# Gate and up projections copied out of PSUM by ACT and multiplied by GpSimd, in place of DVE, in a fused attention and SwiGLU kernel

## The chip, the cores and the metric

One core of one Trainium2 chip. The time is that of the whole kernel on the device, in microseconds (us); lower is better. The engines are TensorE (PE in the profile; its weight loads are PEld), DVE (VectorE), ACT (ScalarE), POOL (GpSimd) and SP (SyncE, which here issues DMAs).

## The reference, cut to what matters

The input is 4 batches of 1024 tokens with 128 channels. A layer norm without weights is shared by an attention branch and a feed-forward branch, and both are added to the input.

```python
xn = (x - mean) / sqrt(var + 1e-5)
# attention: 16 heads of 8 channels, 4 key/value heads, rope, softmax over all 1024 keys
q, k, v = xn @ Wq.T + bq, xn @ Wk.T + bk, xn @ Wv.T + bv
q, k = rope(q), rope(k)
context = softmax(q @ k.T / sqrt(8)) @ v
attention = context @ Wo.T + bo
# feed-forward: weights are integers times 1/127, 384 hidden channels
gate, up = xn @ wg.T, xn @ wu.T
ffn = (silu(gate) * up) @ wd.T
out = x + attention + ffn
```

The kernel forms silu by a tanh: silu(gate) = 0.5 * gate * (1 + tanh(gate / 2)).

## The kernel before

**Groups.** The attention is cut into 16 groups (NG): one batch and one key/value head each, with its 4 query heads. Each group has two passes over the scores. The first finds the maximum of each row: 64 units (AU), each a TensorE matmul of 128 queries by 512 keys into a PSUM bank (`max_unit`, L796) and a DVE reduce out of that bank (`reduce_max`, L640). The second computes the scores transposed, with the negative maxima as extra rows of the matmul (`scores`, L813), takes the exponential on ACT (`exps`, L487) and multiplies by v on TensorE (`weigh`, L882: eight records of a step, called a value batch below).

**Steps.** A group has 16 steps. In a step TensorE issues four max units, which run ahead of their use by 48 units (LEAD), four score matmuls of the next step and one value batch; ACT takes four exponentials; DVE takes four reduces. All engines follow one order written out by hand (`step_order`, L74, from the table `JOB_AT`, L67), in which further jobs are placed:

```python
JOB_AT = {1: (UP, 0), 3: (UP, 1), 5: (NEG_T, 1), 7: (UP, 2), 8: (CTX, 0), 10: (DOWN, 0), 13: (NEG_T, 0), 16: (CTX, 1)}
```

In a step, TensorE's order is max and score matmuls in turn (three of each), the job, the value batch, then the fourth max unit and the fourth score matmul. ACT's order is three exponentials, its part of the job, the fourth exponential.

**The feed-forward jobs.** Each group also does a sixteenth of the feed-forward branch: 256 tokens (CH) and three chunks of 128 hidden channels (FC). UP (`ffn_gate_up`, L888) puts gate in the first and up in the second half of a PSUM bank; ACT writes tanh(gate / 2) to SBUF (L536); DVE's `hidden` (L677 to L684) then makes two instructions that read the bank: gated = (th + 1) * gate (L680) and hid = 0.5 * gated * up (L683). DOWN (`ffn_down_proj`, L897) multiplies the three chunks of hid by the down weights, and DVE adds the result into `y_all` (`add_ffn`, L690).

**The split of the maximum.** When 32 reduces (half a group, HU) are done, DVE negates the row maxima and splits them into three bf16 parts in five small instructions on 128x16 tiles in SBUF, `split_neg`: L651, L655, L657, L660, L662, one behind each of five reduces. L651 has two SBUF inputs. TensorE transposes the parts (`transpose_neg`, L801, job NEG_T), ACT copies them (L478) and SP stores them into the rows of `qc`. The half that job (NEG_T, 1) needs is complete with the fourth reduce of step 3, the one that (NEG_T, 0) needs with the fourth reduce of step 11 (which belongs to the next group).

**Banks.** Jobs and max units share a ring of four PSUM banks (`bank`, L185). Before TensorE takes a bank, `bank_left` (L926) waits for the last reader of what stood in it four places before: for a max unit that is its reduce, for UP it was the second product, `hid_done` (L931). Score matmuls have three banks of their own.

**POOL.** Besides work ahead of the groups, POOL splits the rotated queries of batches 1, 2 and 3 into three bf16 parts: `split_later` (L383 to L405) has seven instructions on 128x1024 tiles in SBUF (L388, L389, L391, L397, L399, L401, L403), and three DMAs (L427) store them. The batches run one behind the other in the loop of L424, beside group 0 and in front of all of POOL's per-group work. That work is `group` (L432): wait for the group's last value batch, then copy v for the group after next (`copy_v`, L411).

**Loops.** Groups 0 to 13 run in a hardware loop of seven iterations with two groups each (even, then odd), so there are six returns to its start. Groups 14 and 15 are written out. The last group has no max units of a next one and does the output projection of the last batches beside it.

Of the kernel before, what the change touches and what calls it, by code (L numbers as in the profile page):

```python
# [16 lines left out]
HID = 384  # L17
# [92 lines left out]
def attention_swiglu(nc, x, wf, wi, biases, bo, tables, identity, out):  # L110
# [3 lines left out]
    with ExitStack() as ctx:  # L114
# [3 lines left out]
        def sem(name):  # L118
            return ctx.enter_context(nc.semaphore(name))
# [31 lines left out]
        neg_max_T = sb("neg_max_T", [PARTS * G * HT, P], BF16)  # L151
        th = sb("th", [P, FC, CH])
        gated = sb("gated", [P, FC, CH])
        hid = sb("hid", [P, FC, CH])
# [92 lines left out]
        ffn_up = sem("ffn_up")  # L247
        tanh_done = sem("tanh_done")
        gated_done = sem("gated_done")
# [123 lines left out]
        def _(pool):  # L373
# [3 lines left out]
            pool.wait_ge(ones_set, 4)  # L377
            pool.sem_inc(q_stored, 1)
            for b, n in ((1, 2), (2, 3)):
                pool.wait_ge(rstd_done, n)  # L380
                normalise(pool, nc.gpsimd, b, xn_done_pool)
# [41 lines left out]

            for b in range(1, B):  # L424
                split_later(b)
                for n in range(PARTS):
                    pool.dma_start(q_parts[b * KV:(b + 1) * KV, :, n, :, :].rearrange("g j d t -> (g j) d t"),  # L427
                                   part[:, (b + 1) % 2, n, :]).then_inc(q_dma, 16)
                pool.wait_ge(q_dma, 16 * PARTS * b)
                pool.sem_inc(q_stored, 2)  # L430

            def group(g, par):  # L432
                pool.wait_ge(pv_done, STEPS * (g + 1) + SLOTS)
                copy_v(g + 2, par)

            with pool.Fori(0, NG // 2 - 1) as pair:
                group(pair * 2, 0)
                group(pair * 2 + 1, 1)


        @block.scalar
        def _(act):
# [83 lines left out]
            def group(g, left):  # L526
                slot = 0
                for s in range(1, STEPS + (left > 1)):
                    after = (g + (s + 1) // STEPS, (s + 1) % STEPS)
                    more = s + 1 < STEPS or left > 1  # L530
                    if more:
                        exps(*after, range(G - 1))
                    for kind, n in step_order(s, left == 1):
                        if kind == UP:
                            act.wait_ge(ffn_up, FC * g + n + 1)
                            nc.scalar.activation(th[:, n, :], bank(slot)[:, 0:CH], ACT.Tanh,  # L536
                                                 scale=0.5).then_inc(tanh_done, 1)
                        if kind == NEG_T:
                            copy_neg(g + 1 - n, n, bank(slot))
                        slot += 1  # L540
                    if more:
                        exps(*after, [G - 1])
                    if s % NT == NT - 1:
                        act.wait_ge(pv_done, STEPS * g + s + 1 + SLOTS)
                        nc.scalar.activation(acc_sb[:, s // NT, :], acc_ps[:, :], ACT.Copy).then_inc(acc_copied, 1)  # L545
# [11 lines left out]
        def _(dve):  # L557
# [75 lines left out]
            dve.wait_ge(ffn_in, 16)  # L633
            nc.vector.tensor_scalar(w_ffn[:, :], wi_sb[:, :], DEQUANT, None, ALU.mult).then_inc(w_done, 1)

# [40 lines left out]

            def hidden(g, c, ps):  # L677

                dve.wait_ge(tanh_done, FC * g + c + 1)
                nc.vector.scalar_tensor_tensor(gated[:, c, :], th[:, c, :], 1.0, ps[:, 0:CH], ALU.add,  # L680
                                               ALU.mult).then_inc(gated_done, 1)
                dve.wait_ge(gated_done, FC * g + c + 1)
                nc.vector.scalar_tensor_tensor(hid[:, c, :], gated[:, c, :], 0.5, ps[:, CH:2 * CH],  # L683
                                               ALU.mult, ALU.mult).then_inc(hid_done, 1)  # L684

            def add_ffn(g, ps):
                dve.wait_ge(bo_added, B)
                dve.wait_ge(ffn_down, g + 1)
                chunk = y_all[:, bass.ds(g * CT, CT), :]
                nc.vector.tensor_tensor(chunk, chunk, ps[:, 0:CT * D].rearrange("p (t d) -> p t d", t=CT),  # L690
                                        ALU.add).then_inc(y_done, 1)
# [20 lines left out]
            def job(g, slot, kind, n):  # L712
                ps = bank(slot)
                if kind == UP:
                    hidden(g, n, ps)
                elif kind == DOWN:
                    add_ffn(g, ps)
# [24 lines left out]
        def _(pe):  # L742
            pe.sem_inc(pv_done, SLOTS)
            pe.wait_ge(w_in, 32)

# [121 lines left out]
            pe.wait_ge(raw_done, 2 * B)  # L867
            pe.wait_ge(w_done, 1)
            pe.wait_ge(qc_loaded[0], DMAS_C)
# [23 lines left out]
            def ffn_down_proj(g, ps):  # L893
                pe.wait_ge(hid_done, FC * (g + 1))
                for t in range(CT):
# [30 lines left out]
            def bank_left(g, kind, n, back=0):  # L926
# [3 lines left out]
                elif kind == UP:  # L930
                    pe.wait_ge(hid_done, FC * g + n + 1 - FC * back)  # L931
                elif kind == DOWN:
# [139 lines left out]
```

## Time and profile before

| | |
|---|---|
| median of 3 runs | 880.38 us |
| lowest and highest | 879.12, 881.32 us |
| the profiled execution | 878.84 us, with a span of 877.0 us |
| busy share of the span | PE 90%, DVE 86%, ACT 68%, PEld 29%, POOL 10% |
| chain that ended last, by engine | PE 61%, DVE 14%, issue 13%, ACT 9% |
| mean granted TensorE clock | 0.953 of full speed |

Times are microseconds from the start of the span unless marked ns. In the timeline a row is one instruction, or several of one group merged (xcount), with its start and its duration; in square brackets stands how long its engine had been idle before it and which engine's instruction released it, where that is known. Merged rows overlap with what runs between their parts. The matmuls are pipelined, so that the durations of neighbours overlap; the distance of two starts says more than a duration. The line number is that of the kernel, and line numbers below are those of the kernel before.

### The profile page before, as it was taken

To read this page: it belongs to the slowest core of one execution; us is meant where nothing else is said; L and a number is where in the kernel's file an instruction comes from. 1 tells how busy PE (TensorE), PEld (TensorE's weight loads), DVE (VectorE), ACT (ScalarE), POOL (GpSimd) and SP (SyncE) were. 2 spreads that over 40 slices of the span, in tenths; PEclk is the share of its full clock that TensorE was granted. 3 is DMA by queue.
4 is the path that set the end of the run, shared out by engine and by line. 5 is a ranking of instruction groups with operands and counts; after the bars stand their busy time and mean duration, and the time that the engine had idled before them with its cause. 6 is when DMAs were issued, how large, how long until landed. Compare 5 with 4: busy or idle time off the path is not lost.

```text
span 877.0 us, 18027 instructions
## 1 busy us (share of the span) xinstructions
PE 790.0 (90%) x4856; PEld 253.0 (29%) x4856; DVE 752.4 (86%) x1486; ACT 595.1 (68%) x1171; POOL 84.2 (10%) x81
## 2 busy tenths in 40 slices
PE   3697699989999899989999899989999899999996
PEld 2221232323322232323322232323223222323252
DVE  7687989979999699979999799979998899999931
ACT  2433477777777577767777577767777677777764
POOL 4169770000000000000000000000000000000000
PEclk9695899999999899999999899989999999999999
DMA  6302222011010101011010000110010000100021
GB/s 194 90 1 63 65 66 64 29 30 27 9 44 6 28 27 28 28 30 27 18 38 6 25 27 28 28 30 27 19 36 9 26 24 27 28 27 2 2 61 37
DMA packets 29220, 30.35 MB, mean 35 GB/s; under 512 B 6672, under 2 KB 21264, under 8 KB 29008
## 3 DMA queue, kind: packets, MB, share of 16 engines
q1 hardware_dynamic: 27552, 25.05, 10.0%
q0 software_dynamic: 720, 2.36, 1.0%
q10 hardware_dynamic: 864, 2.15, 0.7%
q14 instruction: 72, 0.59, 0.2%
q8 instruction: 12, 0.20, 0.1%
HBM read 23.12 MB, written 6.03 MB: 33 GB/s over the span
## 4 chain that ended last, share of the span: by engine, by line
PE 61%; DVE 14%; issue 13%; ACT 9%; SPq 1%; DVEq 1%; DMA 1%; ACTq 1%
PE acc_ps L882 24%; PE banks L796 13%; PE banks L813 8%; DVE mx L640 8%; ACT probs L487 6%; PE banks L888 5%; PE banks L897 3%; PE banks L905 2%; ACT acc_sb L545 2%; DVE neg_max L662 1%; PE banks L922 1%; DVE rest L657 1%; PE banks L801 1%; DVE neg_max L660 1%; PE banks L772 1%
## 5 line engine op out<-in xcount | busy, mean ns | idle before, releaser
L640 DVE TENSOR_REDUCE mx<-banks 128x1 f32<-128x512 f32 x1024 | 639.4, 682 | 56.1 <-PE banks L796 40.5
L487 ACT ACTIVATE probs<-banks 128x512 f32<-128x512 f32 x1024 | 536.9, 603 | 210.4 <-PE banks L813 193.5
L813 PE MATMUL banks<-qc,kc 51*128 51x512 bf16 x1024 | 324.9, 392 | 18.8 <-ACT probs L487 8.7
L796 PE MATMUL banks<-ka,qa 48*128 48x512 bf16 x1024 | 297.7, 394 | 26.6 <-DVE mx L640 11.3
L882 PE MATMUL acc_ps<-probs,v_grp 128*32 128x512 f32 x2048 | 279.8, 619 | 0.7 <-ACT probs L487 0.7
L796 PEld LDWEIGHTS banks<-ka,qa 48*128 48x128 bf16 x1024 | 77.9, 95 | 337.6 <-DVE mx L640 263.2
L813 PEld LDWEIGHTS banks<-qc,kc 51*128 51x128 bf16 x1024 | 79.1, 94 | 134.6 <-ACT probs L487 129.7
L411 POOL COPY v_grp<-v_all 128x64 f32 (+1 forms) x16 | 3.7, 238 | 636.5 <-PE acc_ps L882 636.5
L888 PE MATMUL banks<-xn_T,w_ffn 128*128 (+1 forms) x192 | 57.8, 426 | 0.0
L882 PEld LDWEIGHTS acc_ps<-probs,v_grp 128*32 128x32 f32 x2048 | 40.7, 109 | 57.9 <-issue 47.0
L680 DVE SCALAR_TENSOR_TENSOR gated<-th,banks 128x256 f32<-128x256 f32 x48 | 20.2, 421 | 23.0 <-ACT th L536 19.5
L888 PEld LDWEIGHTS banks<-xn_T,w_ffn 128*128 128x128 f32 x192 | 34.8, 202 | 15.3 <-issue 11.8
L905 PE MATMUL banks<-ident,acc_sb 128*128 128x128 f32 x128 | 20.1, 280 | 7.5 <-ACT acc_sb L545 7.5
L897 PE MATMUL banks<-w_ffn,hid 128*128 128x128 f32 x192 | 25.7, 284 | 0.0
L897 PEld LDWEIGHTS banks<-w_ffn,hid 128*128 128x128 f32 x192 | 22.6, 191 | 3.8 <-issue 3.8
L536 ACT ACTIVATE th<-banks 128x256 f32<-128x256 f32 x48 | 18.4, 383 | 7.6 <-PE banks L888 5.1
L683 DVE SCALAR_TENSOR_TENSOR hid<-gated,banks 128x256 f32<-128x256 f32 x48 | 20.2, 421 | 1.6
L766 PE MATMUL banks<-xn_T,wf_sb 128*128 128x512 f32 x32 | 20.7, 770 | 0.7 <-ACT xn_T L458 0.7
L545 ACT ACTIVATE acc_sb<-acc_ps 128x512 f32<-128x512 f32 x32 | 18.9, 591 | 1.2 <-PE acc_ps L882 1.2
L801 PE MATMUL banks<-ident,neg_max 128*96 128x128 bf16 x32 | 8.2, 257 | 12.2 <-DVE neg_max L662 12.2
L905 PEld LDWEIGHTS banks<-ident,acc_sb 128*128 128x128 f32 x128 | 13.4, 140 | 16.9 <-issue 16.9
L760 PE MATMUL banks<-ident,xn 128*128 128x128 f32 x16 | 4.4, 433 | 14.3 <-DVE xn L278 10.4
(85 smaller groups left out, 270.7 us busy)
## 6 DMA issues: line engine op xcount, KB each, us to landing
qa<-q_parts SPq DMA_DIRECT2D x32, 96.0 KB
qc<-q_parts SPq DMA_DIRECT2D x64, 48.0 KB
q_parts<-part POOLq DMA_DIRECT2D x9, 256.0 KB, 3.8
y_all<-in_x SPq DMA_DIRECT2D x4, 512.0 KB, 9.3
qa<-q_parts SPq DMA_DIRECT2D x32, 64.0 KB
qc<-q_parts SPq DMA_DIRECT2D x64, 32.0 KB
out<-y_all SPq DMA_DIRECT2D x8, 256.0 KB, 2.3
ka<-k_parts SPq DMA_DIRECT2D x32, 48.0 KB
```

What stands on the lines that cost most here:

```text
L487: nc.scalar.activation(probs[:, s % SLOTS, j, :], banks[:, score_bank(G * s + j), :], ACT.Exp, scale=SCALE).then_inc(exp_done, 1)
L545: nc.scalar.activation(acc_sb[:, s // NT, :], acc_ps[:, :], ACT.Copy).then_inc(acc_copied, 1)
L640: nc.vector.tensor_reduce(out=mx[:, h, col, k:k + 1], in_=ps, op=ALU.max, axis=AX.X).then_inc(max_done, 1)
L680: nc.vector.scalar_tensor_tensor(gated[:, c, :], th[:, c, :], 1.0, ps[:, 0:CH], ALU.add, ALU.mult).then_inc(gated_done, 1)
L683: nc.vector.scalar_tensor_tensor(hid[:, c, :], gated[:, c, :], 0.5, ps[:, CH:2 * CH], ALU.mult, ALU.mult).then_inc(hid_done, 1)
L766: return nc.tensor.matmul(s_ps[:, n, h, :], wf_sb[:, c + n * D:c + (n + 1) * D], xn_T[:, b * T + h * W:b * T + (h + 1) * W], start=True, s ...
L796: nc.tensor.matmul(ps, qa[par][rows, j // 2, t * P:(t + 1) * P], ka[par][rows, k * W:(k + 1) * W], start=True, stop=True).then_inc(a_ready, 1)
L813: nc.tensor.matmul(banks[:, score_bank(u), :], kc[par][rows, kt * P:(kt + 1) * P], qc[par][rows, h, j // 2, :], start=True, stop=True).the ...
L882: last = nc.tensor.matmul(acc_ps[VC * j:VC * (j + 1), :], v_grp[par][:, kt, :], probs[:, s % SLOTS, j, :], start=(kt == 0), stop=(kt == NT ...
L888: last = nc.tensor.matmul(ps[:, n * CH:(n + 1) * CH], w_ffn[:, n * HID + c * P:n * HID + (c + 1) * P], xn_T[:, bass.ds(g * CH, CH)], start ...
L897: last = nc.tensor.matmul(ps[:, t * D:(t + 1) * D], hid[:, c, t * P:(t + 1) * P], w_ffn[:, 2 * HID + c * D:2 * HID + (c + 1) * D], start=( ...
L905: last = nc.tensor.transpose(ps[:, t * P:(t + 1) * P], acc_sb[:, h, t * P:(t + 1) * P], ident[:, :])
```

## The change

ACT waits until the hidden tile of the group before is made, then writes its tanh as before, and behind it copies the whole bank (gate and up, 128x512) to a new SBUF tile `gu`. Both count on one semaphore, `gu_done`, and TensorE may take the bank again when both are done. The products move from DVE to POOL as three instructions on 128x256 tiles, all in SBUF: gated = gate * up, th = th * gated, hid = th + gated. The factor 0.5 moves into the dequantised down weights, which makes two DVE instructions of one there. DVE keeps only the add of the down projection. `th` is now written again by POOL.

On POOL, the per-group function now has the three chunks first, then (in groups 0, 1 and 2) one of the batches 1, 2 and 3, then the wait and the copy of v. The first four groups are written out, ten run in a loop of five iterations, and the last two are written out without the copy. `hid_done` and `ffn_down` start from a first count so that the waits for the group before pass in group 0.

```diff
--- before.py
+++ after.py
@@ -150,6 +150,7 @@
         neg_max = sb("neg_max", [P, 2 * 2, PARTS, PAIRS * HT], BF16)
         neg_max_T = sb("neg_max_T", [PARTS * G * HT, P], BF16)
         th = sb("th", [P, FC, CH])
+        gu = sb("gu", [P, FC, 2 * CH])
         gated = sb("gated", [P, FC, CH])
         hid = sb("hid", [P, FC, CH])
         rec = sb("rec", [P, NH, HT, G])
@@ -245,7 +246,7 @@
         pv_done = sem("pv_done")
         acc_copied = sem("acc_copied")
         ffn_up = sem("ffn_up")
-        tanh_done = sem("tanh_done")
+        gu_done = sem("gu_done")
         gated_done = sem("gated_done")
         hid_done = sem("hid_done")
         ffn_down = sem("ffn_down")
@@ -376,6 +377,7 @@
                     nc.gpsimd.memset(kc[i][e * E_ROWS + 32:(e + 1) * E_ROWS, :], 1.0).then_inc(ones_set, 1)
             pool.wait_ge(ones_set, 4)
             pool.sem_inc(q_stored, 1)
+            pool.sem_inc(hid_done, FC)
             for b, n in ((1, 2), (2, 3)):
                 pool.wait_ge(rstd_done, n)
                 normalise(pool, nc.gpsimd, b, xn_done_pool)
@@ -421,7 +423,7 @@
                                         bo_sb[:, :].unsqueeze(1).to_broadcast([P, NT, D]),
                                         ALU.add).then_inc(bo_added, 1)
 
-            for b in range(1, B):
+            def later(b):
                 split_later(b)
                 for n in range(PARTS):
                     pool.dma_start(q_parts[b * KV:(b + 1) * KV, :, n, :, :].rearrange("g j d t -> (g j) d t"),
@@ -429,13 +431,34 @@
                 pool.wait_ge(q_dma, 16 * PARTS * b)
                 pool.sem_inc(q_stored, 2)
 
-            def group(g, par):
-                pool.wait_ge(pv_done, STEPS * (g + 1) + SLOTS)
-                copy_v(g + 2, par)
-
-            with pool.Fori(0, NG // 2 - 1) as pair:
-                group(pair * 2, 0)
-                group(pair * 2 + 1, 1)
+            def hidden(g, c):
+
+                if c == 0:
+                    pool.wait_ge(ffn_down, g + 1)
+                pool.wait_ge(gu_done, 2 * (FC * g + c + 1))
+                nc.gpsimd.tensor_tensor(gated[:, c, :], gu[:, c, 0:CH], gu[:, c, CH:2 * CH],
+                                        ALU.mult).then_inc(gated_done, 1)
+                pool.wait_ge(gated_done, 2 * (FC * g + c) + 1)
+                nc.gpsimd.tensor_tensor(th[:, c, :], th[:, c, :], gated[:, c, :], ALU.mult).then_inc(gated_done, 1)
+                pool.wait_ge(gated_done, 2 * (FC * g + c) + 2)
+                nc.gpsimd.tensor_tensor(hid[:, c, :], th[:, c, :], gated[:, c, :], ALU.add).then_inc(hid_done, 1)
+
+            def group(g, par, batch=None, more=True):
+                for c in range(FC):
+                    hidden(g, c)
+                if batch is not None:
+                    later(batch)
+                if more:
+                    pool.wait_ge(pv_done, STEPS * (g + 1) + SLOTS)
+                    copy_v(g + 2, par)
+
+            for g in range(KV):
+                group(g, g % 2, batch=g + 1 if g + 1 < B else None)
+            with pool.Fori(0, NG // 2 - 3) as pair:
+                group(pair * 2 + KV, 0)
+                group(pair * 2 + KV + 1, 1)
+            group(NG - 2, 0, more=False)
+            group(NG - 1, 1, more=False)
 
 
         @block.scalar
@@ -532,9 +555,11 @@
                         exps(*after, range(G - 1))
                     for kind, n in step_order(s, left == 1):
                         if kind == UP:
+                            act.wait_ge(hid_done, FC * g + n + 1)
                             act.wait_ge(ffn_up, FC * g + n + 1)
                             nc.scalar.activation(th[:, n, :], bank(slot)[:, 0:CH], ACT.Tanh,
-                                                 scale=0.5).then_inc(tanh_done, 1)
+                                                 scale=0.5).then_inc(gu_done, 1)
+                            nc.scalar.activation(gu[:, n, :], bank(slot), ACT.Copy).then_inc(gu_done, 1)
                         if kind == NEG_T:
                             copy_neg(g + 1 - n, n, bank(slot))
                         slot += 1
@@ -631,7 +656,8 @@
             root(slice(2 * NT, NTT), 2)
             nc.vector.tensor_copy(ident16[:, :], ident[:, :]).then_inc(id_done, 1)
             dve.wait_ge(ffn_in, 16)
-            nc.vector.tensor_scalar(w_ffn[:, :], wi_sb[:, :], DEQUANT, None, ALU.mult).then_inc(w_done, 1)
+            for n, scale in ((slice(0, 2 * HID), DEQUANT), (slice(2 * HID, 3 * HID), 0.5 * DEQUANT)):
+                nc.vector.tensor_scalar(w_ffn[:, n], wi_sb[:, n], scale, None, ALU.mult).then_inc(w_done, 1)
 
             def reduce_max(g, a, ps):
                 dve.wait_ge(a_ready, AU * g + a + 1)
@@ -674,18 +700,9 @@
             for a in range(LEAD):
                 maximum(0, a, first_bank(first_slot(a)))
 
-            def hidden(g, c, ps):
-
-                dve.wait_ge(tanh_done, FC * g + c + 1)
-                nc.vector.scalar_tensor_tensor(gated[:, c, :], th[:, c, :], 1.0, ps[:, 0:CH], ALU.add,
-                                               ALU.mult).then_inc(gated_done, 1)
-                dve.wait_ge(gated_done, FC * g + c + 1)
-                nc.vector.scalar_tensor_tensor(hid[:, c, :], gated[:, c, :], 0.5, ps[:, CH:2 * CH],
-                                               ALU.mult, ALU.mult).then_inc(hid_done, 1)
-
             def add_ffn(g, ps):
                 dve.wait_ge(bo_added, B)
-                dve.wait_ge(ffn_down, g + 1)
+                dve.wait_ge(ffn_down, g + 2)
                 chunk = y_all[:, bass.ds(g * CT, CT), :]
                 nc.vector.tensor_tensor(chunk, chunk, ps[:, 0:CT * D].rearrange("p (t d) -> p t d", t=CT),
                                         ALU.add).then_inc(y_done, 1)
@@ -711,9 +728,7 @@
 
             def job(g, slot, kind, n):
                 ps = bank(slot)
-                if kind == UP:
-                    hidden(g, n, ps)
-                elif kind == DOWN:
+                if kind == DOWN:
                     add_ffn(g, ps)
                 elif kind == CTX:
                     normalise_context(g, n, ps)
@@ -741,6 +756,7 @@
         @block.tensor
         def _(pe):
             pe.sem_inc(pv_done, SLOTS)
+            pe.sem_inc(ffn_down, 1)
             pe.wait_ge(w_in, 32)
 
             def transpose_xn(b, h):
@@ -865,7 +881,7 @@
                     pe.wait_ge(max_done, a - 1)
                     transpose_neg(0, 0, first_bank(NEG_BEHIND + 1))
             pe.wait_ge(raw_done, 2 * B)
-            pe.wait_ge(w_done, 1)
+            pe.wait_ge(w_done, 2)
             pe.wait_ge(qc_loaded[0], DMAS_C)
             for j in range(G):
                 scores(0, 0, 0, j)
@@ -891,7 +907,7 @@
                 last.then_inc(ffn_up, 1)
 
             def ffn_down_proj(g, ps):
-                pe.wait_ge(hid_done, FC * (g + 1))
+                pe.wait_ge(hid_done, FC * (g + 2))
                 for t in range(CT):
                     for c in range(FC):
                         last = nc.tensor.matmul(ps[:, t * D:(t + 1) * D], hid[:, c, t * P:(t + 1) * P],
@@ -928,7 +944,7 @@
                 if kind == MAX:
                     pe.wait_ge(max_done, AU * g + n + 1 - AU * back)
                 elif kind == UP:
-                    pe.wait_ge(hid_done, FC * g + n + 1 - FC * back)
+                    pe.wait_ge(gu_done, 2 * (FC * g + n + 1 - FC * back))
                 elif kind == DOWN:
                     pe.wait_ge(y_done, g + 1 - back)
                 elif kind == NEG_T:
```

## Rows read from the trace of the kernel before

**Rows 1.** Timeline, steps 10 and 11 of an odd group: start us, us, instruction, [idle before <-releaser]

```profile
464.04 1.06 PE L882 MATMUL acc_ps<-probs,v_grp 128*32 128x512 f32 x8
...
465.46 3.12 DVE L640 TENSOR_REDUCE mx<-banks 128x1 f32<-128x512 f32 x5 [0.78 <-PE banks L796]
...
466.46 1.06 PE L882 MATMUL acc_ps<-probs,v_grp 128*32 128x512 f32 x8
```

**Rows 2.** Timeline, steps 2 to 5 of that group.

```profile
439.72 1.06 PE L882 MATMUL acc_ps<-probs,v_grp 128*32 128x512 f32 x8
...
443.21 1.07 PE L882 MATMUL acc_ps<-probs,v_grp 128*32 128x512 f32 x8
443.31 0.39 ACT L536 ACTIVATE th<-banks 128x256 f32<-128x256 f32 x1
...
444.63 0.69 DVE L640 TENSOR_REDUCE mx<-banks 128x1 f32<-128x512 f32 x1
...
444.66 2.06 ACT L487 ACTIVATE probs<-banks 128x512 f32<-128x512 f32 x4 [0.96 <-PE banks L813]
...
445.36 0.18 DVE L651 TENSOR_TENSOR row_max<-mx 128x16 f32<-128x16 f32 x1
...
445.63 1.07 PE L882 MATMUL acc_ps<-probs,v_grp 128*32 128x512 f32 x8
446.06 0.17 DVE L655 TENSOR_SCALAR neg_max<-row_max 128x16 bf16<-128x16 f32 x1
...
448.31 0.26 PE L801 MATMUL banks<-ident,neg_max 128*96 128x128 bf16 x1 [0.19 <-DVE neg_max L662]
...
448.50 1.07 PE L882 MATMUL acc_ps<-probs,v_grp 128*32 128x512 f32 x8
```

**Rows 3.** The page's part 5, ACT's copy of a bank: busy, mean ns | idle before.

```profile
L545 ACT ACTIVATE acc_sb<-acc_ps 128x512 f32<-128x512 f32 x32 | 18.9, 591 | 1.2 <-PE acc_ps L882 1.2
```

**Rows 4.** Timeline, step 1 and 2 behind a return of the two-group loop.

```profile
487.23 0.60 ACT L487 ACTIVATE probs<-banks 128x512 f32<-128x512 f32 x1 [1.51 <-PE banks L813]
487.73 0.38 ACT L536 ACTIVATE th<-banks 128x256 f32<-128x256 f32 x1
...
487.99 1.58 ACT L487 ACTIVATE probs<-banks 128x512 f32<-128x512 f32 x3
...
489.07 0.61 PE L796 MATMUL banks<-ka,qa 48*128 48x512 bf16 x1 [0.58 <-DVE hid L683]
```

**Rows 5.** Timeline, group 0 beside POOL's batch 2.

```profile
96.09 2.36 POOL L388 TENSOR_TENSOR xn<-xn,rope 128x1024 f32<-128x1024 f32 x1 [4.89 <-DMA q_parts<-part]
...
96.90 1.58 DVE L651 TENSOR_TENSOR row_max<-mx 128x16 f32<-128x16 f32 x1
...
97.18 1.07 PE L882 MATMUL acc_ps<-probs,v_grp 128*32 128x512 f32 x8
...
99.01 1.78 DVE L655 TENSOR_SCALAR neg_max<-row_max 128x16 bf16<-128x16 f32 x1
...
106.64 1.04 POOL L401 CAST part<-xn 128x1024 bf16<-128x1024 f32 x1
...
107.76 2.12 POOL L403 TENSOR_TENSOR part<-xn,part 128x1024 bf16<-128x1024 f32 x1
...
114.91 1.06 PE L882 MATMUL acc_ps<-probs,v_grp 128*32 128x512 f32 x8
```

**Rows 6.** The page's part 5, POOL's copy of v.

```profile
L411 POOL COPY v_grp<-v_all 128x64 f32 (+1 forms) x16 | 3.7, 238 | 636.5 <-PE acc_ps L882 636.5
```

**Rows 7.** Timeline, ACT and POOL ahead of the groups.

```profile
50.76 1.11 ACT L473 ACTIVATE probs<-banks,bias_sb 128x1024 f32<-128x1024 f32 x1 [1.51 <-PE banks L772]
...
52.03 2.35 POOL L388 TENSOR_TENSOR probs<-probs,rope 128x1024 f32<-128x1024 f32 x1 [18.49 <-ACT probs L473]
```

**Rows 8.** Timeline, row maximum of group 0's other half.

```profile
129.11 0.96 DVE L651 TENSOR_TENSOR row_max<-mx 128x16 f32<-128x16 f32 x1
```

**Rows 9.** Timeline, value batch of step 7, same group as rows 1 and 2.

```profile
454.41 1.06 PE L882 MATMUL acc_ps<-probs,v_grp 128*32 128x512 f32 x8
```

## The prediction

> **What bounds the kernel now.** I read the page's busy shares first: TensorE and DVE both look nearly full, ACT has slack and GpSimd (POOL) is almost idle. Taken alone, that says that any work taken from DVE must pay. So I went to the timeline of single steps. One step of a group ends in a batch of eight value matmuls on TensorE (L882), and I count time from the start of such a batch.
>
> A plain step takes 466.46 - 464.04 = 2.42 us [rows 1]. In that step DVE had been idle for 0.78 us before its first reduce, and the step is no shorter for it. The pace is that of a loop between TensorE and ACT (value batch, score matmul, exponential, the next score matmul). DVE just keeps up with it. A gate/up step takes longer because TensorE has four more matmuls in it (L888), and the change keeps these.
>
> The one place in a group where TensorE waits for DVE is the transpose of the split maximum, L801: idle for 0.19 us, released by L662 [rows 2]. There the step is 448.50 - 445.63 = 2.87 us, and 445.63 is 2.42 after 443.21. From the row maximum (L651) to L662, DVE works without a gap, so what delays one instruction of that chain delays TensorE by as much.
>
> **What the relief of DVE is worth: nothing.** The change takes two DVE instructions a chunk, 48 chunks in all. The best place for this to help is the second gate/up chunk of a group, right ahead of the row maximum. There the reduce starts 444.63 - 443.21 = 1.42 us after the value batch [rows 2]. In the plain step, where DVE was idle and waited for TensorE, it is 465.46 - 464.04 = 1.42 us too [rows 1]. So the reduce is held by its matmul and DVE gains idle time ahead of it, no earlier start. Its bounds are 0 and the 0.45 us (2.87 - 2.42) by which the step exceeds a plain one; I take 0.
>
> **What ACT's copies cost: nothing.** A copy of a whole bank takes 0.591 us (L545) [rows 3]. The instruction behind a tanh starts 487.99 - 487.73 = 0.26 us after it [rows 4]. So tanh at 443.31, copy 443.57 to 444.16; the next exponential starts at 444.66 after 0.96 us of idle time, with its score matmul as the releaser [rows 2]. The cover is 0.5 us. What queues behind the copy is the fourth exponential of the step; without cover its cost would be some 0.5 us a chunk, 24 us in all.
>
> At the six returns of the two-group loop the engines restart late and this cover is absent. There TensorE waited 0.58 us for the old second product, until 489.07 [rows 4]. Now the bank is free at the end of the copy, 488.58, but the copy pushes the fourth exponential from about 488.0 to 488.5, and it ends near 489.1, just when TensorE went on before. Gain and cost cancel: 0. Where fetch stalls fall in the longer ACT loop no row shows; its exponential stood idle for 1.51 us there [rows 4], so I leave half of that, 0.8 us, both ways at each of six returns, 5 us in all, partly in the range. The down projection stands in front of the value batch of step 10, 464.04 - 454.41 = 9.6 us after that of step 7 [rows 1, 9], with nothing but its own matmuls between; POOL will be done 3.5 us after that of step 7: hidden. The dequantisation in two pieces and the 0.5 moved into it lie ahead of the first group and cost nothing that a group waits for.
>
> **What the products on POOL cost DVE.** While POOL worked on SBUF, a DVE instruction on SBUF did not finish before the POOL instruction in flight. L651 ran 1.58 us instead of 0.18 and ended at 98.48; POOL's L388 ended at 98.45. L655, with one SBUF input, ran 1.78 in place of 0.17 [rows 2, 5]. For 128x256 no product is shown. A two-input POOL instruction on 1,024 columns takes 2.36 us, a one-input one 1.04 (L401) [rows 5], a copy of 64 columns 0.238 [rows 6]. The last two give a fixed part of about 0.185 us, so a product costs 0.185 + (2.36 - 0.185)/4 = 0.73 us; without a fixed part it is 0.59. POOL started 52.03 - (50.76 + 1.11) = 0.16 us after the ACT instruction it waited for [rows 7], and L403 starts 0.08 us after the end of L401 [rows 5].
>
> Counted from the value batch of step 3: copy done at 0.95, products at 1.12 to 1.85, 1.93 to 2.66 and 2.74 to 3.47. DVE comes to its row maximum at 445.36 - 443.21 = 2.15 [rows 2]. It meets the second product and waits 0.5 us. Its next split instruction, due 0.70 later, comes at 3.35 and meets the third: 0.1 more. That is 0.6 us a group, all of it in front of L801. In the last group TensorE does other work first, so 15 x 0.6 = **+9.0 us**. The low bound is 0.2 (products of 0.59, first wait only), the high bound 0.95 (the second product starts just ahead of the row maximum, and the third is met too): 3 to 14 us.
>
> For the other direction, what a squeezed-in DVE instruction costs the POOL instruction behind it, I take nothing. The Trainium skill (SBUF — State Buffer, section "SBUF: two separate sides") calls the pair shared by the two engines an exclusive lock held for the whole instruction, on whichever side starts first. By that rule the third product would itself wait for the row maximum and end 0.1 us later, 0.7 us a group or 10.5 us in place of 9.0. No row here shows that half of the rule.
>
> **What moves with the batches.** `later(b)` (seven long POOL instructions and three DMAs) ran back to back in front of POOL's loop. Batch 2 fell on the first split of group 0: the value batches at 97.18 and 114.91 [rows 5] are three steps and 17.73 us apart, where three such steps take 2.87 + 2.42 + 3.49 = 8.78 (the last is a gate/up step, 443.21 - 439.72 [rows 2]). This goes: **-9.0 us**. Batch 3 held another L651 of group 0 for 0.96 instead of 0.17 [rows 8]: **-0.8 us**.
>
> Now each batch starts behind the third chunk of groups 0, 1, 2. The last product ends 3.47 after the value batch of step 7 (that of 454.41 [rows 9]), the batch starts at 3.5. Its L401 runs 10.55 after its start and L403 11.67 [rows 5]: 14.05 to 15.1 and 15.2 to 17.3. The other half's row maximum comes when the five reduces of 465.46 are through, 3.14 us later, at 468.60, or 14.2 [rows 1, 9]. It waits 0.9, the next split instruction 1.5: 2.4 us a group, **+7.2 us** for three. If the row maximum slips in first, it is 2.0, or 6 in all. The three DMAs come behind that; the parts they store are first wanted a group later or more, and the copy of v waits for the group's end as before.
>
> **Sum.** 9.0 + 7.2 - 9.0 - 0.8 = +6.4, say +6.5. The profiled execution took 878.84 us (span 877.0), which becomes 885.3; it lies 0.17% under the median of 880.38. For the median, 880.38 + 6.5 = **886.9 us**. About 0.3% (2.6 us) is what a measurement of this kernel can tell from no change.
>
> **Rivals.**
> - *Short products, slower no more* (0.21). If POOL has hardly a fixed cost, only 0.2 us a group is lost: 3 + 6 - 9.8 = -0.8, and the time is 879 to 882. For it: no row shows the size. Against: the 0.238 us copy of 64 columns.
> - *The relief reaches the split* (0.09), the faster side. If the row maximum could start early enough for L801 never to wait, step 5 would fall to a plain 2.42. It decides once the reduce starts 0.45 us sooner than 1.42 after its value batch. Then 15 x 0.45 = 6.8 is gained in place of 9.0 lost: 7.2 - 9.8 - 6.8 = -9.4, or 871 us. For it: DVE's busy share, and that the old products stood directly ahead of that reduce. Against: the equal 1.42.
> - *ACT becomes the bound* (0.04). If the copy takes more than the 0.96 us that ACT was idle before the fourth exponential, up to 0.5 us is lost 48 times: 887 + 24 = 911. Against: the copy ends 444.16 - 443.70 = 0.46 us into that gap.
>
> **How the numbers follow.** My forecast, with the loss at each split, has 0.66. Its own range is 881 to 894, from the bounds 3 to 14 and 6 to 7.2, with a little for the loop returns. The range of 878 to 894 takes in the short products and leaves out 871, 911 and the far end of the loop returns. Slower by over 0.3% is 0.66: most of the forecast (0.62) and ACT (0.04). Within 0.3% is 0.21: a little of the forecast and most of the short products. Faster is 0.13: the relief, and short products with luck at the loop returns.
>
> **What would show it.** L651 and L655 of each group's first split last longer than 0.2 us, and end together with a POOL product; L801 waits some 0.8 us and step 5 takes about 3.5. Gate/up steps keep 3.49. The stall near 97 us is gone, and three steps 12 to 13 in groups 0 to 2 are over 2 us longer. ACT's idle time before the exponential behind a chunk falls from 0.96 to about 0.5. I am wrong if L651 stays at 0.18, if plain steps drop below 2.42, or if a loop return is over a microsecond longer or shorter.

## The result and the profile after

The changed kernel takes 890.51 us (median of 4 runs, 889.17 to 892.04), the kernel before 879.75 us beside it. The ratio is 1.0122, with a 95% interval of 1.0096 to 1.0147: slower by 1.2%, some 11 us. The forecast was +6.5 us and 886.9 us, with a range of 878 to 894.

The page of the changed kernel, part 1 and three groups of part 5 (busy, mean ns | idle before). The line numbers are now those of the changed kernel: L640 became L666, L651 L677, L655 L681, L662 L688, L796 L812, L801 L817, L882 L898.

```profile
PE 798.4 (90%) x4856; PEld 252.5 (28%) x4856; DVE 719.7 (81%) x1391; ACT 619.0 (70%) x1219; POOL 188.8 (21%) x225
...
L666 DVE TENSOR_REDUCE mx<-banks 128x1 f32<-128x512 f32 x1024 | 639.4, 681 | 119.7 <-PE banks L812 104.4
...
L439 POOL TENSOR_TENSOR gated<-gu 128x256 f32<-128x256 f32 x48 | 34.7, 724 | 372.8 <-ACT gu L562 372.8
...
L562 ACT ACTIVATE gu<-banks 128x512 f32<-128x512 f32 x48 | 28.5, 594 | 0.0
```

DVE was relieved: its busy time fell by 33 us. It spends the relief waiting: the idle time ahead of its reduces rose from 56 to 120 us, and 104 of that end with a TensorE matmul. A product on POOL takes 0.724 us, where the forecast had 0.73.

**Step by step.** I took the start of every value batch from both traces and compared the distances. Step n is the distance from the value batch of step n-1 to that of step n. Nearly all that is different lies in a few places; up to group 14, plain steps (2.42), gate/up steps (3.49), the context step (3.24) and the down step (3.96) are otherwise the same to 0.01 us.

| place | before, us | after, us | sum |
|---|---|---|---|
| step 5 (first split) of groups 1 to 14 | 2.87 | 3.34 | +6.5 |
| step 5 of group 15 | 3.42 | 4.06 | +0.6 |
| steps 5 to 7 of group 0 (old batch 2) | 9.75, 3.73, 4.25 | 3.33, 2.43, 3.48 | -8.5 |
| steps 13 to 15 of group 0 | 3.64, 2.43, 2.64 | 5.13, 3.54, 2.64 | +2.6 |
| steps 13 to 15 of group 1 | 2.87, 2.43, 2.64 | 5.10, 2.86, 3.40 | +3.4 |
| steps 13 to 15 of group 2 | 2.87, 2.43, 2.64 | 5.07, 3.74, 3.72 | +4.6 |
| steps 2 and 3 of the six groups behind a return of the loop | 11.04 | 11.41 | +2.2 |

They add up to 11.4 of the 12.1 us between the two spans (877.0 and 889.1). In group 14 step 5 is 2.92 and 3.39. Of the rest, +0.8 us lies behind the last value batch, +0.1 ahead of the first, and -0.2 in step 8 of group 15 (5.04 against 4.86). That step is the one place outside the returns of the loop where the relief of DVE shows: it is 5.04 or 5.05 in the kernel before, run 8 and both executions of run 4, whose products are on DVE, and 4.86 in all other runs.

**The first split.** Timeline of group 7, steps 3 to 5, the same place as [rows 2].

```profile
449.54 1.07 PE L898 MATMUL acc_ps<-probs,v_grp 128*32 128x512 f32 x8
449.70 0.38 ACT L560 ACTIVATE th<-banks 128x256 f32<-128x256 f32 x1
449.98 0.59 ACT L562 ACTIVATE gu<-banks 128x512 f32<-128x512 f32 x1
...
450.65 0.72 POOL L439 TENSOR_TENSOR gated<-gu 128x256 f32<-128x256 f32 x1 [3.58 <-ACT gu L562]
...
450.96 0.69 DVE L666 TENSOR_REDUCE mx<-banks 128x1 f32<-128x512 f32 x1 [1.00 <-PE banks L812]
...
450.99 2.06 ACT L510 ACTIVATE probs<-banks 128x512 f32<-128x512 f32 x4 [0.42 <-PE banks L829]
...
451.45 0.72 POOL L442 TENSOR_TENSOR th<-th,gated 128x256 f32<-128x256 f32 x1
...
451.68 0.53 DVE L677 TENSOR_TENSOR row_max<-mx 128x16 f32<-128x16 f32 x1
451.96 1.06 PE L898 MATMUL acc_ps<-probs,v_grp 128*32 128x512 f32 x8
...
452.26 0.73 POOL L444 TENSOR_TENSOR hid<-th,gated 128x256 f32<-128x256 f32 x1
...
452.73 0.29 DVE L681 TENSOR_SCALAR neg_max<-row_max 128x16 bf16<-128x16 f32 x1
...
454.35 0.39 PE L812 MATMUL banks<-ka,qa 48*128 48x512 bf16 x1 [0.22 <-DVE mx L666]
...
455.11 0.26 PE L817 MATMUL banks<-ident,neg_max 128*96 128x128 bf16 x1 [0.29 <-DVE neg_max L688]
...
455.29 1.07 PE L898 MATMUL acc_ps<-probs,v_grp 128*32 128x512 f32 x8
```

The reduce ahead of the row maximum starts 1.42 us after the value batch, as before, although DVE had been idle for 1.00 us: the relief buys no earlier start. The row maximum then lasts until POOL's second product ends (451.45 + 0.72 = 452.17, against 451.68 + 0.53 = 452.21). The next split instruction meets the third product (452.99 against 453.02). TensorE then waits for DVE at the transpose, L817 (0.29 us), and already ahead of it, at a max unit (0.22). ACT's copy fits: the exponential behind it starts at 450.99, on its score matmul, after 0.42 us of idle time (0.96 before).

**A batch at the other split.** Timeline of group 1, steps 11 to 14, then, for two stretches, their length, the busy us of PE, PEld, DVE, ACT and POOL, the granted clock, the DMA share and GB/s.

```profile
170.66 1.04 POOL L403 CAST part<-xn 128x1024 bf16<-128x1024 f32 x1
...
170.84 0.89 DVE L677 TENSOR_TENSOR row_max<-mx 128x16 f32<-128x16 f32 x1
171.11 1.06 PE L898 MATMUL acc_ps<-probs,v_grp 128*32 128x512 f32 x8
...
171.78 2.12 POOL L405 TENSOR_TENSOR part<-xn,part 128x1024 bf16<-128x1024 f32 x1
...
172.25 1.68 DVE L681 TENSOR_SCALAR neg_max<-row_max 128x16 bf16<-128x16 f32 x1
...
174.58 0.39 PE L812 MATMUL banks<-ka,qa 48*128 48x512 bf16 x1 [1.81 <-DVE mx L666]
...
176.21 1.07 PE L898 MATMUL acc_ps<-probs,v_grp 128*32 128x512 f32 x8
...
179.07 1.82 PE L898 MATMUL acc_ps<-probs,v_grp 128*32 128x512 f32 x8
```

```profile
171.00:176.00 5.00, 2.56 (x17) 0.54 (x16) 5.00 (x10) 3.17 (x7) 4.42 (x5) 1.00 0.15 29
176.00:180.00 4.00, 3.97 (x25) 0.96 (x25) 3.91 (x7) 2.65 (x6) 0.00 (x0) 0.65 0.52 165
```

POOL's L403 and L405 (the batch's L401 and L403 in the kernel before) hold up L677 and L681, as forecast, and DVE is late by 2.2 us. TensorE waits, 1.81 us at a stretch, and is busy for only 2.56 of 5 us. In the 4 us behind that its granted clock is 0.65 of full speed, so part of the stretch ran at 1.2 instead of 2.4 GHz, and the value batch takes 1.82 instead of 1.07 us. This second loss, in steps 14 and 15, was not in the forecast. It does not follow every such stall. In run 5 below, step 13 of group 0 is 5.41 us long, and steps 14 and 15 behind it keep 2.43 and 2.64. The same view of that step 13 and of the steps behind it in run 5:

```profile
125.80:131.20 5.40, 2.56 (x22) 0.66 (x21) 5.40 (x10) 3.26 (x7) 4.96 (x6) 1.00 0.05 11
131.20:136.20 5.00, 4.96 (x33) 1.24 (x32) 5.00 (x9) 3.56 (x9) 0.24 (x1) 1.00 0.53 155
```

TensorE was no busier in that stall, and the DMA share behind it is as high (0.53 against 0.52), yet the clock stays at 1.00. So the steps are long with the lower clock and not with the DMAs. What decides whether the clock falls is left open.

### The profile page after: what moved, and what is told of

Same layout as the page of the kernel before. It is cut to its first block, busy times and chain, and to the rows that moved or that the text cites. A ratio compares the mean times of both kernels' runs of the same rounds, so it can differ in the third digit from the quotient of the medians.

```text
span 889.1 us, 18214 instructions
## 1 busy us (share of the span) xinstructions
PE 798.4 (90%) x4856; PEld 252.5 (28%) x4856; DVE 719.7 (81%) x1391; ACT 619.0 (70%) x1219; POOL 188.8 (21%) x225
## 4 chain that ended last, share of the span: by engine, by line
PE 59%; DVE 14%; issue 13%; ACT 10%; SPq 1%; DVEq 1%; DMA 1%; ACTq 1%
PE acc_ps L898 24%; PE banks L812 12%; PE banks L829 8%; DVE mx L666 8%; ACT probs L510 7%; PE banks L904 6%; PE banks L913 3%; PE banks L921 2%; ACT acc_sb L570 2%; DVE neg_max L681 1%; PE banks L938 1%; PE banks L817 1%; PE banks L788 1%; PE banks L782 1%; DVE neg_max L686 1%
## 5 line engine op out<-in xcount | busy, mean ns | idle before, releaser
L666 DVE TENSOR_REDUCE mx<-banks 128x1 f32<-128x512 f32 x1024 | 639.4, 681 | 119.7 <-PE banks L812 104.4
L812 PE MATMUL banks<-ka,qa 48*128 48x512 bf16 x1024 | 300.4, 397 | 28.6 <-DVE mx L666 16.5
L898 PE MATMUL acc_ps<-probs,v_grp 128*32 128x512 f32 x2048 | 281.3, 622 | 0.7 <-ACT probs L510 0.7
L812 PEld LDWEIGHTS banks<-ka,qa 48*128 48x128 bf16 x1024 | 78.4, 96 | 349.9 <-DVE mx L666 266.6
L439 POOL TENSOR_TENSOR gated<-gu 128x256 f32<-128x256 f32 x48 | 34.7, 724 | 372.8 <-ACT gu L562 372.8
L898 PEld LDWEIGHTS acc_ps<-probs,v_grp 128*32 128x32 f32 x2048 | 40.7, 109 | 58.3 <-issue 46.0
L904 PEld LDWEIGHTS banks<-xn_T,w_ffn 128*128 128x128 f32 x192 | 35.7, 207 | 15.9 <-issue 12.5
L444 POOL TENSOR_TENSOR hid<-th,gated 128x256 f32<-128x256 f32 x48 | 35.1, 731 | 3.8
L442 POOL TENSOR_TENSOR th<-th,gated 128x256 f32<-128x256 f32 x48 | 34.8, 724 | 3.8
L562 ACT ACTIVATE gu<-banks 128x512 f32<-128x512 f32 x48 | 28.5, 594 | 0.0
L817 PE MATMUL banks<-ident,neg_max 128*96 128x128 bf16 x32 | 8.2, 257 | 12.2 <-DVE neg_max L688 12.2
```

Source lines behind the costliest of these rows:

```text
L439: nc.gpsimd.tensor_tensor(gated[:, c, :], gu[:, c, 0:CH], gu[:, c, CH:2 * CH], ALU.mult).then_inc(gated_done, 1)
L442: nc.gpsimd.tensor_tensor(th[:, c, :], th[:, c, :], gated[:, c, :], ALU.mult).then_inc(gated_done, 1)
L444: nc.gpsimd.tensor_tensor(hid[:, c, :], th[:, c, :], gated[:, c, :], ALU.add).then_inc(hid_done, 1)
L666: nc.vector.tensor_reduce(out=mx[:, h, col, k:k + 1], in_=ps, op=ALU.max, axis=AX.X).then_inc(max_done, 1)
L812: nc.tensor.matmul(ps, qa[par][rows, j // 2, t * P:(t + 1) * P], ka[par][rows, k * W:(k + 1) * W], start=True, stop=True).then_inc(a_ready, 1)
L898: last = nc.tensor.matmul(acc_ps[VC * j:VC * (j + 1), :], v_grp[par][:, kt, :], probs[:, s % SLOTS, j, :], start=(kt == 0), stop=(kt == NT ...
```

## Experiments

Each run has the kernel before beside it on the same chip, in three sets: its median was 882.07 us in that of runs 1 to 4, 879.66 in that of runs 5 and 6, and 881.98 in that of runs 7, 8 and the two repetitions. The changed kernel itself is in none of these sets, so a run is compared with it through the two ratios to the kernel before.

**1. The second chunk's products wait for the split.** On the changed kernel:

```diff
                 pool.wait_ge(gu_done, 2 * (FC * g + c + 1))
+                if c == 1:
+                    pool.wait_ge(neg_step, NEG * NH * (g + 1))
```

> The changed kernel, in which POOL begins the products of the second chunk only when DVE has finished the split of the row maximum. Theory (the products hold up DVE's small split instructions): step 5 of every group falls from 3.33 back to 2.87 us, 16 x 0.46 = 7 us less than the changed kernel's 890.5, so about 883. Rival (step 5 is longer because ACT or the new order of the bank's release is late): step 5 stays at 3.33 and the time at 890. The down projection still finds its hidden tiles ready; were it late, step 10 would exceed 3.96.

Measured: 883.55 us, ratio to the kernel before 1.0012 (0.9993 to 1.0031). Timeline of group 7:

```profile
449.25 0.18 DVE L679 TENSOR_TENSOR row_max<-mx 128x16 f32<-128x16 f32 x1
...
451.99 0.16 DVE L690 TENSOR_TENSOR neg_max<-rest,neg_max 128x16 bf16<-128x16 f32 x1
...
452.23 0.73 POOL L441 TENSOR_TENSOR gated<-gu 128x256 f32<-128x256 f32 x1 [7.59 <-DVE neg_max L690]
```

The row maximum is back at 0.18 us and step 5 at 2.87 in groups 0 to 13 (2.92 in group 14 and 3.42 in group 15, as in the kernel before). The down step keeps 3.96. Steps 13 to 15 of groups 0 to 2 stay long (5.10, 3.40, 2.81 in group 0). So the products alone made step 5 longer, and ACT had no part in it: its copies are still there. By the ratios (1.0122 and 1.0012) the run gives back 9.7 us, by the steps 7; the ratios are not sharp enough to tell these apart.

**2. The batches between the two splits.** On the changed kernel, `split_later` is cut in two: its three rope instructions run behind the first split and ahead of the third chunk, its other four and the DMAs behind the third chunk.

```diff
                 for c in range(FC):
+                    if c == FC - 1 and batch is not None:
+                        pool.wait_ge(neg_step, NEG * NH * (g + 1))
+                        split_later(batch, (0,))
                     hidden(g, c)
```

> The changed kernel, in which the batches 1 to 3 on POOL lie between the two splits of groups 0, 1 and 2: three instructions before the third chunk, four behind it. Theory: steps 13 to 15 of these groups (11.4 us over a plain group, of which 4.7 us fall in steps 14 and 15, behind the stall) come back to 2.87, 2.43 and 2.64, so about 879. Rival (steps 14 and 15 are long for the load of other DMAs, not for the stall): only the 6.7 us of step 13 go and the time is about 884.

Measured: 879.58 us, ratio 0.9972 (0.9952 to 0.9992). Steps 13 to 15 of groups 0, 1 and 2 are 2.87, 2.42 and 2.64 us; step 5 stays at 3.34. The long steps 14 and 15 went with the stall in step 13, although the same DMAs are still issued, which is against the rival; run 5's group 0, shown above, is more direct evidence against it.

**3. Both edits.**

> Both edits of the two runs before on the changed kernel. Theory: the two losses add up, 890.5 - 7.4 - 11.4 = about 871.5. Rival (POOL's instructions only move and hit something else): 878 or more.

Measured: 870.65 us, ratio 0.9869 (0.9844 to 0.9895), and once more (the last set) 870.74 us, 0.9890 (0.9866 to 0.9915). The two losses add up: by the ratios, 1.1% and 1.5% alone, 2.3 to 2.5% together. This version beats both kernels.

**4. The kernel before, with only its batches moved.** Products stay on DVE. POOL's group loop is split to make room for the batches (four groups written out, ten in a loop).

```diff
-            for b in range(1, B):
+            def later(b):
                 split_later(b)
...
+            for g in range(KV):
+                if g + 1 < B:
+                    pool.wait_ge(neg_step, NEG * NH * (g + 1))
+                    later(g + 1)
+                group(g, g % 2)
```

> The kernel before, products on DVE, with nothing changed but the place of the batches on POOL, between the two splits of groups 0, 1 and 2. Theory: the stall of group 0 goes (9.7 us, forecast and seen in the changed kernel) and nothing else changes, so about 870.5, the same as or slightly better than the run with products on POOL and both edits, since the relief of DVE is worth nothing. Rival (the relief of DVE is worth something that the collisions hid): this kernel is slower than that run by 3 us or more.

Measured: 872.06 us, ratio 0.9887 (0.9861 to 0.9913). And in the set with the repetition of run 3:

> The run with both edits once more, on the same chip as the next one. Theory: products on POOL and products on DVE give the same time once nothing collides, so the two ratios differ by less than 0.3%. Rival: the relief of DVE or the copies on ACT show, one way or the other.

> The kernel before with the batches between the splits once more, on the same chip as the run before this one. The same 0.3% as there.

There it was 871.33 us, ratio 0.9882 (0.9859 to 0.9905), against 0.9890 for products on POOL. The two versions can't be told apart, in either set: the medians differ by 1.4 and 0.6 us, within the spread of six runs each. What is gained over the kernel before comes from the place of the batches alone.

**5. No products at all.** The kernel before without L680 and L683; the hidden tile stays zero, so the feed-forward branch is missing from the output. TensorE may take the bank again once the tanh is done.

```diff
-                if kind == UP:
-                    hidden(g, n, ps)
-                elif kind == DOWN:
+                if kind == DOWN:
...
-                pe.wait_ge(hid_done, FC * (g + 1))
+                pe.wait_ge(tanh_done, FC * (g + 1))
```

> The kernel before without its 96 DVE products: the hidden tile stays zero, so the feed-forward branch is left out of the result. TensorE may take the bank once the tanh is done. This is the most that taking work from DVE can give. Theory (DVE only keeps up): steps keep 2.42, 2.87 and 3.49 us and the only gain is at the six returns of the loop, where TensorE waited for the second product, up to 0.6 us each: 877 to 880. Rival (DVE paces the steps): a gate/up step would lose up to 0.9 us of its 3.49, 48 times, and the time would come down to 840 to 860.

Measured: 874.93 us beside 879.66, ratio 0.9949 (0.9927 to 0.9971), 4.7 us less and below the 877 to 880 that I expected. The plain, split and gate/up steps of groups 1 to 14 are 2.43, 2.87 and 3.48 us: the products on DVE pace none of them. Their absence pays behind the returns of the loop (steps 2 and 3 there: 10.58 us, mean of six, against 11.04 in the kernel before, 2.8 us in all). In group 0 it comes to nothing: step 5 is shorter (8.40 against 9.75), step 13 longer (5.41 against 3.65), and the group is 0.2 us shorter in all. Another 1.6 us between the two profiled executions lie ahead of the first value batch, whose start differs from run to run by more than that (81.6 to 84.5).

**6. The same with ACT's copies.** TensorE waits for both the tanh and the copy.

```diff
+                            nc.scalar.activation(gu[:, n, :], bank(slot), ACT.Copy).then_inc(tanh_done, 1)
```

> The run without products, with ACT's copy of the whole bank behind each tanh put in (the copy is not read, the feed-forward branch is left out). It prices ACT's part of the change alone. Theory: hidden in the steps, 0 to 3 us more than without the copies, all of it in steps 2 and 3 of even groups, behind a return of the loop. Rival (the copies delay the fourth exponential everywhere): 24 us more.

Measured: 881.03 us, ratio 1.0022 (1.0005 to 1.0038), 6.1 us more than without the copies, twice what I expected at most. Between the two profiled executions there are 5.6 us: 4.0 behind the returns (11.25 against 10.58, six times), 0.9 in group 0, and the rest, 0.7, is +0.9 behind the last value batch and -0.3 ahead of the first. That tail takes 9.4 us in run 3, which has the copies too, and in the kernel before, and 10.3 here, so it is not theirs. In all other steps the copies are hidden, to 0.01 us. So at the returns the copies take back what the absence of DVE's products gives, and the forecast's "gain and cost cancel" holds to a few us only.

**7. A POOL instruction that only writes.** In the changed kernel the second product becomes a fill of a scratch tile; the factor 1 + tanh is left out of the hidden tile.

```diff
-                nc.gpsimd.tensor_tensor(th[:, c, :], th[:, c, :], gated[:, c, :], ALU.mult).then_inc(gated_done, 1)
+                nc.gpsimd.memset(scratch[:, :], 0.0).then_inc(gated_done, 1)
```

> The changed kernel, in which POOL's second product of each chunk is replaced by a fill of a scratch tile of about the same duration, which writes SBUF and reads nothing (so the hidden tile is not the reference's: the factor 1 + tanh is left out of it). It tells apart what holds DVE. If any POOL instruction in flight holds DVE's split instructions, the row maximum (L677 there) still lasts about 0.53 us. If only a POOL instruction that reads SBUF holds a DVE instruction with two SBUF inputs, it is back at 0.17 us, and the wait is met one instruction later or not at all.

Measured: 886.09 us in a single execution, beside 881.98; what is read here is its trace. Timeline of group 7:

```profile
447.10 0.76 POOL L442 MEMSET scratch<- 128x800 f32 x1
447.47 0.17 DVE L677 TENSOR_TENSOR row_max<-mx 128x16 f32<-128x16 f32 x1
447.56 0.69 DVE L666 TENSOR_REDUCE mx<-banks 128x1 f32<-128x512 f32 x1
447.95 0.73 POOL L444 TENSOR_TENSOR hid<-th,gated 128x256 f32<-128x256 f32 x1
448.17 0.54 DVE L681 TENSOR_SCALAR neg_max<-row_max 128x16 bf16<-128x16 f32 x1
```

The row maximum, with its two inputs in SBUF, lies wholly inside the fill and takes its usual 0.17 us, 0.18 at most, in all 16 groups. L681 then meets the third product, which reads SBUF, and lasts until that ends (448.71 against 448.68). Step 5 is 3.24 us. The Trainium skill (SBUF — State Buffer, "SBUF: two separate sides") says just this of a DVE instruction with two SBUF inputs: it meets the lock only against a GpSimd instruction that reads SBUF. The trace agrees. This trace also has one case of a DVE instruction with one SBUF input against the fill: in group 15 L681 starts inside it, takes 0.22 instead of 0.17 us and ends 0.03 behind it, so it seems to be held where the row maximum is not. One case, 0.05 us long, does not settle that.

**8. The first chunk in step 2.** On the kernel of run 4:

```diff
-JOB_AT = {1: (UP, 0), 3: (UP, 1), 5: (NEG_T, 1), 7: (UP, 2), 8: (CTX, 0), 10: (DOWN, 0), 13: (NEG_T, 0), 16: (CTX, 1)}
+JOB_AT = {2: (UP, 0), 3: (UP, 1), 5: (NEG_T, 1), 7: (UP, 2), 8: (CTX, 0), 10: (DOWN, 0), 13: (NEG_T, 0), 16: (CTX, 1)}
```

> The kernel before with the batches between the splits, and the first gate/up chunk one step later, in step 2 instead of step 1, away from the place where ACT and DVE restart behind a return of the loop. Theory (TensorE waits there for the chunk's second product, 0.6 us at six returns): up to 3 us less than the same kernel with the chunk in step 1. Rival (the restart of ACT is all that counts there): no difference.

Measured: 873.28 us, ratio 0.9911 (0.9884 to 0.9937), against 0.9882 for the chunk in step 1 in the same set: no gain, more likely a small loss. Timeline behind the return at group 8:

```profile
481.60 2.56 ACT L492 ACTIVATE probs<-banks 128x512 f32<-128x512 f32 x5 [1.44 <-PE banks L818]
...
483.28 2.08 PE L893 MATMUL banks<-xn_T,w_ffn 128*128 x4
...
485.28 1.94 PE L887 MATMUL acc_ps<-probs,v_grp 128*32 128x512 f32 x8
```

ACT's late restart is still there, and the chunk's four matmuls now fall in the slow stretch behind it and take 2.08 us. At the usual pace they take 1.13. Steps 2 and 3 there take 13.2 us (mean of six), of which 1.06 is the chunk; without it they are some 0.8 us longer than in run 4's repetition (11.33).

## Why the prediction was right, and where it was off

- **Direction and mechanism: right, and shown.** Of the loss two parts stand clear: POOL's products against the first split (run 1 takes them away) and POOL's batches against the other (run 2 does). With both gone the time is under that of the kernel before (run 3), and it is the same whether the products lie on POOL or on DVE (runs 3 and 4).
- **Relief of DVE, forecast 0: right in the steps.** The equal 1.42 us before and after, and run 5, show it. Behind the returns it is worth 2.8 us by the profiled execution of the kernel before, and more by those of run 4; the forecast named this gain and set it against the copies. The +2.2 us of the table there is within the spread: single returns lie between 10.3 and 12.5 us, and the two profiled executions of run 4, whose products are still on DVE, have means of 11.51 and 11.33. The forecast's sign of being wrong, a return over a microsecond longer or shorter, is therefore no test: the first return went from 10.36 to 12.11 us, but two executions of one kernel (run 3) also have 10.72 and 12.38 there.
- **First split, forecast 0.6 us for 15 groups (+9.0): 0.46 to 0.47 in groups 0 to 14, 0.64 in the last, 7.6 in all.** The product's length (0.73) and start (1.12 us after the value batch, measured 450.65 - 449.54 = 1.11) were right. I let the row maximum wait for POOL's end and then run its whole 0.17 us. It ended 0.04 us behind the product, so the waiting covers most of its own time: 0.36 instead of 0.5. The other direction, taken as nothing, did not show: the third product starts 0.08 us behind the second, as POOL's instructions do elsewhere, and takes 0.73. The waiting forecast at the transpose, 0.8 us, came as 0.29 there and 0.3 at the max units ahead. Group 15, which I left out, has no reduces between its split instructions and lost the most.
- **The batches' new place, forecast 2.4 us for three groups (+7.2): 11.4.** Step 13 alone lost 2.2 to 2.3 us a group, as worked out. The other 4.7 us lie in steps 14 and 15, behind the stall. This is the term that failed, and its own bounds of 6 to 7.2 as well. The rows of group 0 had shown it: there, too, two long steps stood behind the long one (the granted clock was 0.67 in them), and I counted them for what goes away (-9.0) and not for what comes. The time lies within the forecast range because of room left for another term (the first split was given up to 14 us and took 7.6), which is luck.
- **The old collisions, forecast -9.0 and -0.8: -9.0 and -0.8** (17.73 us to 9.24, less the 0.46 of the new split loss; step 13 had 0.77 over its usual).
- **ACT's copies, forecast 0: right in the steps,** with 0.42 us left of the 0.96 (0.5 forecast); off by a few us at the returns (run 6).
- **Sum.** 7.6 + 11.4 - 9.0 - 0.8 + 2.2 = 11.4 us between the profiled executions, against a forecast of 6.5. The medians differ by 10.8 us. The first split, 1.4 us less than forecast, hides a third of what the batches cost more.

## What to carry to other kernels

An engine that is 86% busy is not therefore the one that sets the pace: look at a step in which it had been idle just before, and see whether that step is shorter. GpSimd's idle time is not free for the taking where DVE works on small tiles in SBUF on the critical path; place GpSimd's work by the clock of those instructions, or make it wait for them, as here, where one wait and the moved batches were worth more than 2% against the changed kernel. And when a stall of TensorE is added to a sum, ask what the steps behind it will take: here that was between nothing (run 5) and 2.4 us (group 2) for stalls of about the same length.

## What the runs showed of the hardware

- A DVE instruction that is held by a GpSimd instruction ends some 0.04 us after it, not a whole instruction length after it (452.21 against 452.17, 453.02 against 452.99).
- The row maximum, with two SBUF inputs, is held only by a GpSimd instruction that reads SBUF: 0.17 us inside a fill, 0.53 beside a product.
- After a stretch in which TensorE was busy for 2.56 of 5 us, the granted clock of the next 4 us was 0.65 (group 1 of the changed kernel). After 2.56 of 5.4 us in group 0 of run 5 it was 1.00 over the next 5 us. A half-idle TensorE can be followed by the lower clock and need not be.
